# The third layer norm cut in two parts and laid between the last expert groups of a four-stage tower

## What is computed

```python
h = _L0_tok_ref(x, L0_tok_W, L0_tok_b)
h = h + _L0_attn_ref(_layernorm(h), ...)
h = h + _L0_ffn_ref(_layernorm(h), ...)      # 16 experts, two of them weighted per token
h = h + _L1_attn_ref(_layernorm(h), ...)     # attention by L1 distance
h = h + _L1_ffn_ref(_layernorm(h), ...)      # two routed layers of 128x128

def _layernorm(x, axis=-1, eps=1e-05):
    m = jnp.mean(x, axis=axis, keepdims=True)
    v = jnp.var(x, axis=axis, keepdims=True)
    return (x - m) / jnp.sqrt(v + eps)

# _L0_ffn_ref: every expert is computed for every token
h1 = jnp.einsum('bsd,edh->bseh', x, w1)
h2 = jnp.einsum('bsd,edh->bseh', x, w2)
hidden = jax.nn.silu(h1) * h2
expert_out = jnp.einsum('bseh,eho->bseo', hidden, w3)
return jnp.einsum('bseo,bse->bso', expert_out, dispatch)

# _L1_attn_ref
v = (x @ wqv_w.T + wqv_b).reshape(b, t, 3 * h, d)
q, vf, vb = (v[:, :, :h], v[:, :, h:2 * h], v[:, :, 2 * h:])
k = x[:, :, None, :] * wk[None, None]
a = _l1_scores(q, k)                         # -sum_w |q - k| / sqrt(w)
a = jax.nn.softmax(jnp.concatenate([a, zeros]), axis=1)[:, :t]
o = (bf + bb).sum(axis=2)                    # a with vf and with vb
y = o * jax.nn.sigmoid(1.702 * o)
return x + (y @ fanin_w.T + fanin_b)
```

## Time and profile before

| | |
|---|---|
| median of 3 runs | 2432.77 us (2432.23 to 2436.34) |
| profiled execution | 2433.18 us, span 2431.3 us |
| PE busy | 2149.1 us (88%) |
| DVE busy | 2071.3 us (85%) |
| POOL busy | 1766.5 us (73%) |
| ACT busy | 1573.1 us (65%) |

### The profile page before, as it was taken

How to read it: one execution, slowest core, us unless ns; L and a number is a source line. 1 busy time by engine, 2 the same in 40 slices (tenths; PEclk the granted TensorE clock), 3 DMA queues, 4 the chain that set the end, 5 groups by cost and what they waited for, 6 DMA issues and landing times.

```text
span 2431.3 us, 48360 instructions
## 1 busy us (share of the span) xinstructions
PE 2149.1 (88%) x13399; PEld 1011.8 (42%) x13399; DVE 2071.3 (85%) x2497; ACT 1573.1 (65%) x4028; POOL 1766.5 (73%) x1033
## 2 busy tenths in 40 slices
PE   5566999999749999999999999999999999999978
PEld 3352333333213444444444444444444444444457
DVE  2877777777879999999999999999999999999974
ACT  1333343343328877877878777787777778777756
POOL 0111333333439999999999999999999999999943
PEclk8787999999869999999999999999999999999979
DMA  4302333233212221222212222122221222212201
GB/s 125 81 1 49 80 76 74 69 78 80 49 30 56 56 56 47 56 52 56 55 49 56 50 56 55 49 56 51 56 55 48 55 52 55 56 47 55 52 20 33
DMA packets 169426, 135.47 MB, mean 56 GB/s; under 512 B 45661, under 2 KB 151070, under 8 KB 169247
## 3 DMA queue, kind: packets, MB, share of 16 engines
q1 hardware_dynamic: 159850, 118.02, 19.6%
q10 hardware_dynamic: 9532, 16.91, 2.9%
HBM read 10.51 MB, written 4.19 MB: 6 GB/s over the span
## 4 chain that ended last, share of the span: by engine, by line
POOL 60%; PE 18%; DVE 11%; issue 5%; ACT 3%; POOLq 1%; ACTq 1%; DMA 1%; DVEq 0%; SPq 0%
POOL absd L1671 57%; PE pp L658 3%; DVE absd L1493 3%; POOL attk L1682 3%; PE pp L683 1%; PE pp L951 1%; PE pp L679 1%; DVE score L1553 1%; ACT absd L1080 1%; PE pp L684 1%; PE pp L680 1%; ACTq L1067 1%; DVE yw L1477 1%; PE pp L582 1%; PE pp L640 1%
## 5 line engine op out<-in xcount | busy, mean ns | idle before, releaser
L1553 DVE TENSOR_REDUCE score<-pp 128x16 f32<-128x1024 f32 x1280 | 1481.3, 1213 | 131.7 <-PE pp L851 131.6
L1671 POOL TENSOR_TENSOR absd<-absd 128x2560 f32<-128x2560 f32 x635 | 1447.1, 2279 | 68.3 <-ACT absd L1147 24.3
L851 PE MATMUL pp<-blocks,pick 128*128 128x512 f16 x2560 | 737.9, 381 | 28.7 <-DVE score L1553 20.7
L1147 ACT ACTIVATE absd<-pp 128x512 f32<-128x512 f32 x1280 | 695.5, 598 | 66.7 <-PE pp L839 54.4
L839 PE MATMUL pp<-blocks,pick 128*128 128x512 f16 x1280 | 416.0, 383 | 42.3 <-ACT absd L1147 26.9
L1638 POOL TENSOR_TENSOR absd<-absd,yw 128x512 f32<-128x512 f32 x112 | 142.2, 1270 | 307.0 <-DVE yw L1477 307.0
L851 PEld LDWEIGHTS pp<-blocks,pick 128*128 128x128 f16 x2560 | 206.7, 97 | 345.8 <-DVE score L1553 235.0
L1080 ACT ACTIVATE absd<-pp 128x512 f32<-128x512 f32 x256 | 149.5, 597 | 203.4 <-PE pp L680 156.7
L1493 DVE SCALAR_TENSOR_TENSOR absd<-pp,absd 128x512 f32<-128x512 f32 x256 | 171.6, 686 | 81.2 <-ACT absd L1080 68.3
L839 PEld LDWEIGHTS pp<-blocks,pick 128*128 128x128 f16 x1280 | 113.7, 97 | 281.1 <-ACT absd L1147 177.7
L1177 ACT ACTIVATE expd<-attn 128x65 f32<-128x65 f32 x512 | 160.8, 328 | 0.0
(11 more groups left out here) (229 smaller groups left out, 2682.3 us busy)
## 6 DMA issues: line engine op xcount, KB each, us to landing
blocks<-qk SPq DMA_DIRECT2D x1032, 64.0 KB, 2.0
blocks<-gT SPq DMA_DIRECT2D x128, 128.0 KB
blocks<-gT ACTq DMA_DIRECT2D x128, 128.0 KB
attn<-score SPq DMA_DIRECT2D x256, 64.0 KB, 2.1
xs<-xn SPq DMA_DIRECT2D x66, 32.0 KB, 1.8
big<-in_wrb_t SPq DMA_DIRECT2D x1, 2064.0 KB
big<-in_x_rows SPq DMA_DIRECT2D x4, 512.0 KB, 6.3
token_rows<-big SPq DMA_DIRECT2D x8, 256.0 KB, 2.0
```

Source lines behind the costliest of these rows:

```text
L851: mm = pe.matmul(ps[bank + n], pick[:, unit % 8 + n, :], blocks[:, b, unit // 16, unit // 8 % 2, :], start=True, stop=True)
L1147: nc.scalar.activation(absd[odd][:, 16 * u + 8 * n:16 * u + 8 * n + 8, :], ps[4 + n].rearrange("p (h w) -> p h w", w=D), ACT.Abs).then_inc ...
L1553: dve.tensor_reduce(score[:, odd, b, 16 * d:16 * d + 16], pp[:, bank:bank + 2, :].rearrange("p n (h w) -> p (n h) w", w=D), AX.X, ALU.add, ...
L1671: nc.gpsimd.tensor_tensor(x[:, :, 0:w], x[:, :, 0:w], x[:, :, w:2 * w], ALU.add).then_inc(X["tree"], 1)
```

## The change

The third layer norm, `layernorm_mid`, has two parts. Part 0 covers pairs 0 to 47 in chunks of 16 and is a generator of sixteen pieces, which VectorE's groups 12 to 15 call in given slots: (4, 5, 6, 7), then (0, 1, 2, 4, 5, 7), then (0, 1, 3, 4, 5, 6), then none. A piece is one wide operation over 16 pairs, some with a small one behind it; the piece in slot 3 of group 14 is the five small operations behind the root. Part 1 covers pairs 48 to 63 and follows the last `add_up`. ScalarE takes the root of part 0 in slot 2 of group 14 and of part 1 behind group 15.

Groups 12 to 15 are written out on VectorE, 14 and 15 on the other engines. Group 15 has no gating and no turn for a group behind it. In their place stand the first pair's `turn` (slot 1), `queries` (4), `low` (5), `keys` (6) and `low` (7), with ScalarE's copies. SP loads the first pair before the gates of group 15 and fills `blocks` behind the last `weigh`. L1's constants are made after the token rows, from three loads that stand ahead of those rows on SP; `wk_b` lies in `attk` instead of `big`. GpSimd adds to `wc` in eight parts in slots 4 to 7 of groups 0 and 1, and `xn` to `h` in four parts, three of them in group 15. In the diff, definitions that moved with their text (`turn`, `queries`, `keys`, `low`, `prepare_x`, `high_q`, `high_k`, `load_pair`) are left out.

```diff
+        MID_AT = (slice(0, 48), slice(48, PAIRS))
...
+        def layernorm_mid(dve, c):
+            step, n, at = ln_step[2], MID * c, MID_AT[c]
+            squares2 = big[:].rearrange("p (n d) -> p n d", d=D)
+            chunks = [slice(k, k + 16) for k in range(at.start, at.stop, 16)]
+            m = len(chunks)
+            total, mean, var, sd, r, t = (stat[:, k, at] for k in range(6))
+            dve.wait_ge(C["sum"], at.stop // 4)
+            for x in chunks:
+                dve.tensor_reduce(stat[:, 0, x], h[:, x, :], AX.X, ALU.add).then_inc(step, 1)
+                if x.stop < at.stop:
+                    yield
...
+            for x in chunks:
+                dve.tensor_tensor(xn[:, x, :], h[:, x, :], stat[:, 1, x].unsqueeze(2).to_broadcast(wide), ALU.subtract).then_inc(step, 1)
+                yield
+            for k, x in enumerate(chunks):
+                dve.wait_ge(step, n + k + 1)
+                dve.tensor_tensor(squares2[:, x, :], xn[:, x, :], xn[:, x, :], ALU.mult).then_inc(step, 1)
+                yield
+            for k, x in enumerate(chunks):
+                dve.wait_ge(step, n + k + 1)
+                dve.tensor_reduce(stat[:, 0, x], squares2[:, x, :], AX.X, ALU.add).then_inc(step, 1)
+                if x.stop < at.stop:
+                    yield
...
+            yield
+            dve.wait_ge(ln_sd[2], c + 1)
+            dve.reciprocal(r, sd).then_inc(step, 1)
...
+            yield
+            for x in chunks:
+                op = dve.tensor_tensor(xn[:, x, :], xn[:, x, :], stat[:, 4, x].unsqueeze(2).to_broadcast(wide), ALU.mult)
+                if x.stop < at.stop:
+                    op.then_inc(step, 1)
+                else:
+                    op.then_inc(xn_ready[2], 1)
+                yield
...
+            sp.wait_ge(pads, PADS)
+            sp.dma_start(wk_b, a["L1_attn_wk"].partition_broadcast(D)).then_inc(X["wk_in"], 16)
+            sp.dma_start(wqv[0:D, :], a["wqv_t"]).then_inc(X["wk_in"], 16)
+            sp.dma_start(wqv[D:D + 1, :], a["L1_attn_wqv_b"].unsqueeze(0)).then_inc(X["wk_in"], 16)
...
-            with sp.Fori(1, G4 // 2) as i:
+            with sp.Fori(1, G4 // 2 - 1) as i:
+            spread_gates(G4 - 2, 0, False)
             sp.wait_ge(xn_ready[2], 1)
-            sp.dma_start(wk_b, a["L1_attn_wk"].partition_broadcast(D)).then_inc(X["wk_in"], 16)
+            load_pair(slice(0, 1))
+            spread_gates(G4 - 1, 1, False)
...
+            sp.wait_ge(C["yw"], 8 * G4)
             fill_blocks(0, 0, True)
             load_pair(slice(1, 2))
             for q in range(4):
+                if q == 1:
+                    sp.wait_ge(xn_ready[2], 2)
                 pair(q, q % 2, q, slice(q + 2, q + 3))
...
+                    if last:
+                        if k == 1:
+                            pe.wait_ge(C["gT"], G4)
+                            turn(0, 0)
+                        if k == 2:
+                            moe_sum(g - 1, 1 - b, g + 1)
+                        if k == 4:
+                            pe.wait_ge(X["consts"], 3)
+                            pe.wait_ge(C["sum"], G4 - 1)
+                            queries(0, 0)
+                        if k == 5:
+                            low(0, 0, 0)
+                        if k == 6:
+                            keys(0, 0)
+                        if k == 7:
+                            low(0, 0, 1)
+                        continue
...
-            with pe.Fori(1, G4 // 2) as i:
+            with pe.Fori(1, G4 // 2 - 1) as i:
+            moe_group(G4 - 2, 0, False)
+            moe_group(G4 - 1, 1, False, last=True)
             moe_down(8 * G4 - 1, 7, False)
-            moe_sum(G4 - 1, 1, G4 + 1)
-            pe.wait_ge(l1_in, L1_IN)
-            pe.wait_ge(C["sum"], G4)
-            pe.wait_ge(C["gT"], G4 + 1)
...
+            def middle_root(c):
+                act.wait_ge(ln_step[2], (MID_VAR[0], MID + MID_VAR[1])[c])
+                at = MID_AT[c]
+                nc.scalar.activation(stat[:, 3, at], stat[:, 2, at], ACT.Sqrt).then_inc(ln_sd[2], 1)
+            def moe_group(g, b, first, root=False, last=False):
                 act.wait_ge(C["gT"], g + 1)
...
+                    if root and k == 2:
+                        middle_root(0)
+                    if last:
+                        if k == 1:
+                            prepare_x(0, 0)
+                        if k == 4:
+                            high_q(0, True)
+                        if k == 5:
+                            low(0, 0)
+                        if k == 6:
+                            high_k(0)
+                        if k == 7:
+                            low(0, 1)
+                        continue
...
+            dve.wait_ge(attn_in, ATTN_IN)
+            dve.wait_ge(X["wk_in"], 16 * 3)
+            dve.memset(wk_diag[D:KA], 0.0)
+            dve.tensor_scalar(neg_eye[:], ident[:], -LO_SCALE, None, ALU.mult).then_inc(X["consts"], 1)
+            dve.tensor_scalar(wqv[:, 0:QK], wqv[:, 0:QK], LO_SCALE, None, ALU.mult).then_inc(X["consts"], 1)
+            dve.scalar_tensor_tensor(out=wk_diag[0:D], in0=wk_b, scalar=LO_SCALE,
+                                     in1=ident[0:D, 0:D].unsqueeze(1).to_broadcast([D, HEADS, D]),
+                                     op0=ALU.mult, op1=ALU.mult).then_inc(X["consts"], 1)
...
-                    if k == 0:
+                    if k == 0 and not final:
                         low_x(g + 1, 1 - b)
-                    if k == 2:
+                    if k == 2 and not final:
                         gates = gating(g + 1, 1 - b)
                         next(gates)
                     if k == 3 and at >= 1:
                         add_up(g - 1, last)
-                    if k == 7:
+                    if k == 7 and not final:
                         for _ in gates:
                             pass
+                    if k in pieces:
+                        next(norm)
...
-            with dve.Fori(1, G4 // 2) as i:
+            with dve.Fori(1, G4 // 2 - 2) as i:
+            norm = layernorm_mid(dve, 0)
+            for g, pieces in ((G4 - 4, (4, 5, 6, 7)), (G4 - 3, (0, 1, 2, 4, 5, 7)), (G4 - 2, (0, 1, 3, 4, 5, 6)), (G4 - 1, ())):
+                moe_group(g, g % 2, slice(4 * g - 4, 4 * g), 2, norm, pieces, g == G4 - 1)
             weigh(G4 - 1, 1, 7, 2)
             add_up(G4 - 1, slice(4 * G4 - 4, 4 * G4))
-            dve.wait_ge(C["sum"], G4)
-            layernorm_dve(dve, 2)
-            dve.memset(wk_diag[D:KA], 0.0)
-            dve.tensor_scalar(neg_eye[:], ident[:], -LO_SCALE, None, ALU.mult).then_inc(X["consts"], 1)
-            dve.wait_ge(l1_in, L1_IN)
...
+            def add_shared(n):
+                if n == 0:
+                    pool.wait_ge(mlp_in, MLP_IN)
+                    for l in range(2):
+                        nc.gpsimd.tensor_tensor(ws[:, l, 0:HID], ws[:, l, 0:HID], ident[:], ALU.add).then_inc(wc_ready, 1)
+                    pool.wait_ge(wc_ready, 2)
+                l, e = n // 4, slice(4 * (n % 4), 4 * (n % 4) + 4)
+                nc.gpsimd.tensor_tensor(wc[:, l, e], wc[:, l, e], ws[:, l, :].unsqueeze(1).to_broadcast([P, 4, HID + 1]),
+                                        ALU.add).then_inc(wc_ready, 1)
+            def add_x(c):
+                x = slice(16 * c, 16 * c + 16)
+                nc.gpsimd.tensor_tensor(h[:, x, :], h[:, x, :], xn[:, x, :], ALU.add).then_inc(X["hx"], 1)
...
+                    if first and k >= 4:
+                        add_shared(4 * b + k - 4)
+                    if last:
+                        if k == 2:
+                            pool.wait_ge(xn_ready[2], 1)
+                        if k in (2, 4, 6):
+                            add_x(k // 2 - 1)
...
+            moe_group(G4 - 2, 0, None)
+            moe_group(G4 - 1, 1, None, last=True)
             pool.wait_ge(l1_in, L1_IN)
-            for l in range(2):
-                nc.gpsimd.tensor_tensor(ws[:, l, 0:HID], ws[:, l, 0:HID], ident[:], ALU.add).then_inc(wc_ready, 1)
-            pool.wait_ge(wc_ready, 2)
-            for l in range(2):
-                nc.gpsimd.tensor_tensor(wc[:, l], wc[:, l], ws[:, l, :].unsqueeze(1).to_broadcast([P, EXPERTS, HID + 1]),
-                                        ALU.add).then_inc(wc_ready, 1)
-            pool.wait_ge(xn_ready[2], 1)
-            nc.gpsimd.tensor_tensor(h[:], h[:], xn[:, 0:PAIRS, :], ALU.add).then_inc(X["hx"], 1)
+            pool.wait_ge(xn_ready[2], 2)
+            add_x(3)
```

179 lines of the change are left out of this document (94 added, 85 removed).

## The result

The changed kernel takes 2405.3 us (median of 4 runs, 2402.49 to 2407.05), the kernel before 2432.5 us on the same chip. The ratio is 0.9887, with a 95% interval of 0.9868 to 0.9905. A second set of runs of the same changed kernel, on another chip, gave 2405.9 us and 0.9887 (0.9870 to 0.9903). The gain is 27.2 us, and the time lies 2.9 us above the forecast.

What follows compares the result with a forecast made beforehand. GpSimd's attention add tree was taken as a fixed block, so its start counts. Terms -42.1 + 9.9 + 1.1 + 1.2 - 0.5 = -30.4 us from 2433.18 gave 2402.8, as median 2402.4 us; range 2394 to 2414.

Steps and rivals of the forecast that it cites:

- The handover: Last `add_up` to the attention's first reduce: 7.7 us for 49.8, so -42.1 us; VectorE late next, not the fill.
- The pieces: Sixteen norm pieces in groups 12 to 14: free in VectorE's gaps, otherwise paid at 1.15 us each; +9.9 us net.
- I give them 1.2 us: Allowance in groups 12 to 14 for two-input pieces in slots 0, 2 and 3 blocked by GpSimd: 1.2 us.
- The saving of the written-out groups: Groups 12 to 14 on VectorE without the loop's register instructions: three groups save 3.3 us.
- The last group and its tail: Group 15 to `add_up`: gating saves at least 1.1 us, products even with transposes, GpSimd's add costs 2.2; +1.1 us.
- Groups 0 and 1: GpSimd's adds to `wc` between the accumulates there block VectorE's gating: +1.2 us, ends 0 and 3.
- The start of the attention: First reduce to GpSimd's first batch, 9.6 us: two units ready beforehand save some, -0.5 us.
- A sign that spoke against me: Attention from GpSimd's first batch to end stays at 1715 us within 1 us; wrong if that length changes.
- the first rival: Pieces in groups 12 to 14 hide better, every gap used, blocks vanish: pieces +5, total -36, 2396 us; chance 0.16.
- second: Pieces paid in full, each two-input piece also waits for GpSimd: +22 for +9.9, total -18.3, 2414 us; chance 0.12.
- third: First pair's work holds up the last group, with a late fill 8 us: total -22, 2410 us; chance 0.08.
- fourth: TensorE's clock falls to 1.2 GHz in groups 12 to 14: up to +75 us, slower, 2440 us; chance 0.04.

Runs made afterwards that it cites:

- x12: Changed kernel with three norm parts, all engines written out, GpSimd waits and adds moved, pieces in slots 0, 6, 7 of groups 8 to 14: 2381.54 us.
- x13: x12 with nothing in slot 0: pairs 0 to 47 as three parts of 16, pieces in slots 6 and 7: 2378.37 us.
- x3: Changed kernel with GpSimd's third add of 16 pairs moved behind the last accumulate: 2399.87 us, ratio 0.9870.
- x2: Changed kernel with the first pair of the attention made behind the last group again: 2409.04 us, ratio 0.9901.
- x4: Changed kernel without the sixteen pieces (norm of pairs 0 to 47 and its root left out): 2396.19 us, ratio 0.9854.

## Why the prediction was right

The time, 2405.3 us, is within the range and 2.9 us from the forecast. Step by step:

- **The handover** was forecast at 7.7 us for 49.8 and came at 8.0. The five passes take 1.22 to 1.23 us each, for 1.15. VectorE was late next and not the fill: there is no idle time before the first reduce. The constants cost nothing where they stand.
- **The pieces.** The mechanism held (gaps absorb, slots 3 to 5 pay), and the term was mis-sized: 13.2 us gross, 8.9 to 9.6 measured. The groups 12, 13 and 14 grew by 0.6, 3.0 and 2.8 us instead of 2, 3 and 4, counted from one group's first `hid` to the next. The step that failed is "I give them 1.2 us" for the block: pieces delay the gating's small operations past GpSimd's accumulates, which gives back 2.8 us, while 1.7 us of new blocks come. That is 1.1 us less for 1.2 us more, so 2.3 us; the other 1.3 to 2.0 us of the miss stay open. The saving of the written-out groups is nearly right: 78.2 for 81.1 us without pieces, so 2.9 us for 3.3.
- **The last group and its tail** came at +1.3 us for +1.1, by errors that cancel. The products of the first pair are not even with what they replace, they cost 1.6 to 2.3 us; GpSimd's add costs 2.3 to 3.0 us, not 2.2. So, by what is left of the sum, leaving out the gating and the transposes gave back 2.6 to 4 us (1.6 to 2.3 and 2.3 to 3.0, less 1.3) and not the 1.1 I set "at the least".
- **Groups 0 and 1** cost 0.4 us of the 1.2.
- **The start of the attention** is 9.7 us where it was 9.6: two units ready beforehand save nothing, for GpSimd waits 7.17 us for ScalarE's absolute values.
- **What the sum did not have**: +2.6 us in groups 2 to 11 and +1.2 us for `h`, which change between executions (the second profile has +0.7 and -0.1), and +2.7 us in the L1 experts, which belong to the program. VectorE was ahead of GpSimd by 0.23 us at one of these multiplies before and is behind it by 0.08 us now, and so one more multiply of 1.22 us stood for 3.34. That is 2.1 of the 2.7 us.
- **A sign that spoke against me.** I had said that I am wrong if the length of the attention from GpSimd's first batch to the end, 1715 us, changes by more than 1 us. These 1715 us reach to the end of the program (2431.3 less 716.25) and so hold the L1 experts too; now they are 1718.8 (2405.1 less 686.32). The attention alone kept to 1.0 us, the stage behind it did not, and I had set it at nothing without a reason.
- **Luck.** The whole came out closer than its parts. The pieces cost 3.6 us less than I forecast, while groups 2 to 11, `h`, the attention and the L1 experts, which the sum had at 0, brought 7.5 us.
- **The rivals.** The pieces lay between the forecast and the first rival's value. None was paid in full (second); the third was partly at work, 1.6 to 2.3 us and not 8; the granted clock in groups 12 to 14 stayed at 1.00, so the fourth had nothing:

```profile
549.23:577.41 28.18, 26.17 (x120) 9.18 (x117) 25.09 (x50) 11.09 (x21) 9.77 (x8) 1.00 0.31 75
577.41:608.38 30.97, 27.30 (x124) 9.45 (x124) 28.71 (x51) 11.09 (x21) 11.30 (x9) 1.00 0.29 68
608.38:639.10 30.72, 26.05 (x116) 8.63 (x112) 28.25 (x56) 13.67 (x23) 11.72 (x8) 1.00 0.29 68
```

## What to carry to other kernels

Work that fills idle time is free only in the slots where the idle time is: in x12 two pieces cost at most 0.3 us a group behind the last operation of a chain (in x13 up to 1.1), and a further one in slot 0 another 1.3 to 1.9 us. When a group loses the work of one engine, look which engine sets its pace next, for what is put in there is then paid by that one. And where VectorE and GpSimd start two operations within 0.1 us of each other, order them by a wait: it was worth 3 to 4 us here by the medians, and costs one changed line.

## What was not expected of the hardware

- The register instructions of a loop cost 0.7 to 0.9 us in a group of some 28 us on VectorE, and 0.2 us more on the other engines together.
- An operation of 0.2 us with one input in memory also stands until GpSimd's instruction is through: `neg_eye` 8.30 us beside `h += xn` and 0.23 us alone, `mean` 2.32 and 3.18 us and 0.17 us alone. The reduce at 656.84 beside the same `wc` add did not wait.
- ScalarE's issue of two transfers takes 1.33 or 1.79 us in the same place of the same program, and the group follows with 27.5 or 28.0 us.
- TensorE's granted clock in the first 13 us behind the attention was 0.58 before and 0.69 after; in the kernels whose programs are the changed kernel's from there on it was 0.60 (x3) to 0.75 (x2, x4). In the five kernels with the moved bias wait it was 0.58, 0.69, 0.76, 0.90 and 0.90, and the stage took 106.4, 104.2, 102.0, 102.1 and 102.1 us. What decides it stays open.
